# Folding a two-layer network's weights on one core: last pieces by block, and the next stage's first tiles made early

## What is computed

```
h  = gate(LN(x))                        # sigmoid, tanh and cosine of two 512x512 products
for l in 0, 1:
    h = LN(h + (h @ ent_w[l] + ent_b[l]) @ ent_pw[l] + ent_pb[l])       # 512x2048, 2048x512
    h = LN(h + sum_p (h @ path_w[l,p] + path_b[l,p]) * cos/sin factor(phase[l,p]))
```

## Time and profile before

| what | value |
|---|---|
| median of 3 runs | 1646.76 us (1643.83 to 1646.97) |
| the profiled execution: time | 1646.83 us |
| the profiled execution: span | 1644.8 us |
| PE busy | 1490.0 us (91%) |
| PEld busy | 1129.7 us (69%) |
| DVE busy | 1124.7 us (68%) |
| ACT busy | 809.7 us (49%) |
| POOL busy | 539.5 us (33%) |
| mean granted PE clock | 0.956 of 2.4 GHz |

### The profile page before, as it was taken

How to read it: one execution, slowest core, us unless ns; L and a number is a source line. 1 busy time by engine, 2 the same in 40 slices (tenths; PEclk the granted TensorE clock), 3 DMA queues, 4 the chain that set the end, 5 groups by cost and what they waited for, 6 DMA issues and landing times. The chain is left out here.

```text
span 1644.8 us, 26366 instructions
## 1 busy us (share of the span) xinstructions
PE 1490.0 (91%) x8136; PEld 1129.7 (69%) x8136; DVE 1124.7 (68%) x1815; ACT 809.7 (49%) x1723; POOL 539.5 (33%) x593
## 2 busy tenths in 40 slices
PE   4799999999946999999999987999799499898998
PEld 3577777777635777777777766888444278777876
DVE  6788778887526878787878753777558535555556
ACT  4566665566434555555555533555201355545554
POOL 4235324341024554545454513221051331402021
PEclk9899999999977999999999997999899699999999
DMA  4123334324257544454454414000354000000000
GB/s 152 64 90 95 105 107 127 100 84 114 82 174 242 123 115 116 106 124 109 122 108 116 132 27 168 0 0 1 128 204 154 0 1 1 1 27 0 26 26 26
DMA packets 140505, 143.77 MB, mean 87 GB/s; under 512 B 83488, under 2 KB 103072, under 8 KB 138784
## 3 DMA queue, kind: packets, MB, share of 16 engines
q1 hardware_dynamic: 138720, 133.87, 28.2%
q10 hardware_dynamic: 1728, 9.20, 1.7%
HBM read 113.54 MB, written 29.49 MB: 87 GB/s over the span
## 5 line engine op out<-in xcount | busy, mean ns | idle before, releaser
L942 ACT ACTIVATE c_e_t_high<-c_et_ps 128x512 fp32r<-128x512 f32 x128 | 76.7, 599 | 227.4 <-PE c_et_ps L1011 227.4
L820 POOL TENSOR_TENSOR c_mixed_low<-c_whole,c_mixed_high 128x512 fp32r<-128x512 f32 x64 | 96.0, 1500 | 177.1 <-ACT c_mixed_high L954 177.1
L77 DVE TENSOR_TENSOR b_rot_parts_low<-b_rot,b_rot_parts_high 128x1536 fp32r<-128x1536 f32 x64 | 136.0, 2125 | 21.9 <-ACT b_rot_parts_high L526 21.9
L1003 PE MATMUL c_sc_ps<-c_kv_t,c_q 128*128 128x257 f32 x512 | 136.6, 391 | 13.7 <-DMA c_q<-carried_queries 13.7
L843 DVE TENSOR_REDUCE c_peak<-c_sc_ps 128x2 f32<-128x514 f32 x128 | 88.5, 692 | 55.0 <-PE c_sc_ps L1003 54.3
L264 POOL TENSOR_TENSOR b_turned_raw<-b_turn_part 128x384 f32<-128x384 f32 x32 | 70.1, 2189 | 167.7 <-DVE b_key_parts_low L77 166.5
L1003 PEld LDWEIGHTS c_sc_ps<-c_kv_t,c_q 128*128 128x128 f32 x512 | 99.6, 196 | 33.1 <-DMA c_q<-carried_queries 14.6
L309 DVE TENSOR_TENSOR b_rot<-b_w_qr,b_angle 128x1536 f32<-128x1536 f32 x64 | 119.2, 1863 | 0.2
L1515 PE MATMUL f_ps<-f_right,f_left 128*128 128x512 f32 x256 | 112.5, 601 | 7.3 <-POOL spare L1487 5.0
L934 ACT ACTIVATE c_e<-c_sc_ps,c_peak 128x257 f32<-128x257 f32 x256 | 118.8, 475 | 0.0
L70 PE MATMUL c_out_ps<-c_w_vo_high,c_mixed_high 128*128 128x512 f32 x256 | 112.0, 437 | 3.3 <-POOL c_mixed_low L820 3.3
(11 more groups left out here) (211 smaller groups left out, 3876.3 us busy)
## 6 DMA issues: line engine op xcount, KB each, us to landing
c_q<-carried_queries SPq DMA_DIRECT2D x64, 256.0 KB, 3.7
c_ends_spread<-end_weights SPq DMA_DIRECT2D x64, 256.0 KB, 4.3
carried_queries<-x SPq DMA_DIRECT2D x7, 2048.0 KB, 11.2
b_early<-early SPq DMA_DIRECT2D x15, 640.0 KB, 3.9
c_raw<-cache_t SPq DMA_DIRECT2D x64, 128.5 KB, 3.8
c_swapped<-cache_t SPq DMA_DIRECT2D x128, 64.2 KB, 3.8
f_left<-ent_in SPq DMA_DIRECT2D x16, 512.0 KB, 5.5
f_right<-ent_out SPq DMA_DIRECT2D x16, 512.0 KB, 6.7
```

Of the source, the lines that this page charges most:

```text
L77: return nc.vector.tensor_tensor(low, value, high.bitcast(F32), ALU.subtract)
L820: nc.gpsimd.tensor_tensor(mixed[1][:, w, :, u], whole[:, u % 2].rearrange("p (h s) -> p h s", h=H), mixed[0][:, w, :, u].bitcast(F32), ALU ...
L1003: last = nc.tensor.matmul(sc_ps[:, 2 * half + c, 0:L], q[:, u, at], kv_t[:, u], start=True, stop=True)
```

## The change

Seven edits:

1. The block `root_deviations` for x2 is gone; ACT's root and DVE's inverse are the first instructions of `fold_weights`.
2. In `fold_weights`, PE does pieces 0 to 5 as before, and pieces 6 and 7 block by block: for each m the four last steps k, then a signal `block_done`. ACT copies a block when it is done, and copy and rounding alternate block by block. DVE's `finish` starts on a block when that block is copied, and makes the low part of block m - 1 behind the three instructions of block m. PE starts block m of layer 1 when block m of layer 0 is copied. The slots of pieces 6 and 7 come free with the fourth `block_done`.
3. The six bias rows are no longer spread over 128 partitions and added at the end. POOL clears `acc` (128 x 2048), SP then loads each row into one partition of `acc` (six DMAs of 2 KB), and PE's spreading matmul adds them with the rest. Four of them are multiplied by their phase row on one partition (DVE, 1 x 512 each) ahead of the second half of layer 0's sum. `keep_bias` is one copy. DVE's first sum step now waits for the root and for all six rows, the first step is a multiply-add like the others, and the two memsets of `acc` are gone.
4. Only the four phase rows are spread (1 MB).
5. POOL normalises the four tiles of the feed-forward's first turn at the start of the fold (eight instructions of 128 x 512), ahead of its wait for `modulated`.
6. In the feed-forward the input tiles come first on ACT and DVE, and the gate weights are rounded and split in eight blocks of 128 x 4 x 128; each gate result waits only for its own block. The tanh starts behind all eight splits.
7. A tile of the self attention shares the memory of `bias`; the tile `e_xn` lives since before the fold.

The core of the diff:

```diff
 SP, fold_weights
-            sp.dma_start(row[:] ..., rows[0:NR] ... .to_broadcast([P, NR * D])).then_inc(rows_loaded, 16)
+            sp.wait_ge(cleared, 1)
+            for j, at, r in places:
+                sp.dma_start(acc[at:at + 1, j], rows[r:r + 1]).then_inc(rows_loaded, 16)
+            sp.dma_start(phases[:] ..., rows[PH:PH + MODS] ... .to_broadcast([P, MODS * D])).then_inc(phases_loaded, 16)
...
-                        sp.wait_ge(piece_used, turn - SLOTS + 1)
-                        sp.wait_ge(accumulated, (turn - SLOTS + 1) * KQ)
+                        old = turn - SLOTS
+                        if old % PIECES < WHOLE:
+                            sp.wait_ge(piece_used, WHOLE * (old // PIECES) + old % PIECES + 1)
+                        else:
+                            sp.wait_ge(block_done, CD * (old // PIECES + 1))
+                        sp.wait_ge(accumulated, (old + 1) * KQ)
 POOL, fold_weights
-            nc.gpsimd.memset(ones, 1.0).then_inc(pool_chained, 1)
+            nc.gpsimd.memset(acc, 0.0).then_inc(cleared, 1)
+            nc.gpsimd.memset(ones, 1.0).then_inc(ones_set, 1)
+            pool.wait_ge(inverted, 1)
+            gate.normalise_first(nc, pool, x2, stat)
             pool.wait_ge(modulated, 1)
 PE, fold_weights
-            pe.wait_ge(pool_chained, 1)
             for l in range(LAYERS):
-                for q in range(PIECES):
+                for q in range(WHOLE):
...
+                for m in range(CD):
+                    for k in range(WHOLE * KQ, CF):
+                        if m == 0 and k % KQ == 0:
+                            arrived(l, k // KQ)
+                        last = multiply(l, k, m)
+                    last.then_inc(block_done, 1)
 ACT, fold_weights
+            nc.scalar.activation(stat[:, 1], stat[:, 1], ACT.Sqrt, bias=eps[:], scale=1.0 / D).then_inc(rooted, 1)
...
             for n, j in enumerate(STAGES):
-                if j % 2 == 0:
-                    act.wait_ge(piece_used, PIECES * (j // 2 + 1))
-                    for m in range(CD):
+                for m in range(CD):
+                    if j % 2 == 0:
+                        act.wait_ge(block_done, CD * (j // 2) + m + 1)
                         nc.scalar.activation(raw[:, 0, m], ps[:, m], ACT.Copy).then_inc(copied, 1)
-                for m in range(CD):
                     act.wait_ge(gained, CD * n + m + 1)
                     nc.scalar.activation(folded[0][:, j, m], raw[:, j % 2, m], ACT.Copy).then_inc(rounded, 1)
 DVE, fold_weights (order at the start)
+            dve.wait_ge(rooted, 1)
+            nc.vector.reciprocal(stat[:, 1], stat[:, 1]).then_inc(inverted, 1)
             dve.wait_ge(loads.col_loaded, 16)
+            dve.wait_ge(rows_loaded, 16 * len(places))
             sum_entangled(0, range(SLOTS * KQ))
-            dve.wait_ge(rows_loaded, 16)
+            dve.wait_ge(phases_loaded, 16)
...
+            for l in range(LAYERS):
+                for p in range(PW):
+                    at = slice(32 * p, 32 * p + 1)
+                    nc.vector.tensor_tensor(acc[at, 2 * l + 1], acc[at, 2 * l + 1], phases[at, l * PW + p], ALU.mult).then_inc(rows_weighed, 1)
+            dve.wait_ge(rows_weighed, MODS)
             sum_entangled(0, range(SLOTS * KQ, CF))
 feed_forward
-            normalise_tiles(0)
             normalise_tiles(1)
...
-                if f == 0:
-                    pe.wait_ge(weights_split, which + 1)
+                pe.wait_ge(weights_split, r + 1)
...
-            round_weights(0, angle)
             for u in range(G):
                 round_input(0, u)
-            round_weights(1, sigma)
+            for which, raw in enumerate((angle, sigma)):
+                for f in range(CD):
+                    round_weights(which, f, raw)
             act.wait_ge(preset, 1)
-            act.wait_ge(weights_split, 2)
+            act.wait_ge(weights_split, 2 * CD)
```

More of the change, by code:

```diff
@@ L1432, in first, with fold_weights @@
         sp.dma_start(self.paths[:], self.path[0]).then_inc(self.paths_loaded, 16)
-def fold_weights(nc, loads, path, rows, spare, half_pi, ident, folded, bias, out_norm, gate):
-    PB, PH = LAYERS, LAYERS + LAYERS * PW
+def fold_weights(nc, loads, path, rows, x2, stat, eps, spare, half_pi, folded, bias, out_norm, ident, gate):
+    PH = LAYERS + LAYERS * PW
     with ExitStack() as ctx:
@@ L1448, in fold_weights @@
         raw = sb("f_raw", [P, 2, CD, D])
-        turns = raw[:, 0, 0:LAYERS * PW]
-        row = sb("f_row", [P, NR, D])
+        turns = raw[:, 0, 0:MODS]
+        phases = sb("f_phases", [P, MODS, D])
         acc = spare[:, 0:2 * LAYERS * D].rearrange("p (j d) -> p j d", j=2 * LAYERS)
@@ L1454, in fold_weights @@
         bias_ps = ctx.enter_context(nc.psum_tensor("f_bias_ps", [P, 2 * LAYERS, D], F32))
[L1455 to L1459, removed]
+        phases_loaded, norm_loaded, rows_loaded, rows_weighed = (sem(f"f_{n}") for n in ("phases_loaded", "norm_loaded", "rows_loaded", "rows_weighed"))
+        ones_set, cleared, rooted, inverted, pool_chained, summed = (
+            sem(f"f_{n}") for n in ("ones_set", "cleared", "rooted", "inverted", "pool_chained", "summed"))
+        chained, cosined, modulated, piece_used, block_done, copied = (
+            sem(f"f_{n}") for n in ("chained", "cosined", "modulated", "piece_used", "block_done", "copied"))
+        accumulated, spread, gained, rounded, split = (sem(f"f_{n}") for n in ("accumulated", "spread", "gained", "rounded", "split"))
         block = ctx.enter_context(nc.Block())
@@ L1500, in _, with multiply @@
         def _(pe):
+            def multiply(l, k, m):
+                slot = k % (SLOTS * KQ)
+                if l and k == 0:
+                    pe.wait_ge(copied, CD * (l - 1) + m + 1)
+                return nc.tensor.matmul(ps[:, m], left[:, slot, m * P:(m + 1) * P], right[:, slot], start=k == 0, stop=k == CF - 1)
             def spread_bias(j, n):
@@ new lines, in _ @@
+            dve.wait_ge(loads.col_loaded, 16)
+            dve.wait_ge(rows_loaded, 16 * len(places))
+            sum_entangled(0, range(SLOTS * KQ))
+            dve.wait_ge(phases_loaded, 16)
+            flat = lambda a: a.rearrange("p r d -> p (r d)")
+            link(nc.vector.tensor_scalar(phases[:], phases[:], PI / 4, None, ALU.subtract))
+            link(nc.vector.tensor_scalar(turns, phases[:], 1.0 / (2 * PI), MAGIC, ALU.mult, ALU.add))
+            link(nc.vector.tensor_scalar(turns, turns, MAGIC, None, ALU.subtract))
@@ L1646, in feed_forward @@
         minus_quarter = sb("e_minus_quarter", [P, 1])
-        xn = sb("e_xn", [P, G, D])
+        xn = gate.tiles
         xn_t = pair("e_xn_t", [P, CD, T])
@@ L1934, in _ @@
             dve.wait_ge(loaded, 48)
-            split_weights(0, angle)
             for u in range(G):
                 split_input(0, u)
-            split_weights(1, sigma)
+            for which, raw in enumerate((angle, sigma)):
+                for f in range(CD):
+                    split_weights(which, f, raw)
             apply_gates(0)
@@ L2010, in perceiver_block @@
             loads = FoldLoads(nc, fold_scope, paths, ent_in, ent_out, path, columns)
[L2011 to L2013 removed]
+            self_attention(nc, x1, stat, holo, basis_t, bias, ident, loads)
+            fold_weights(nc, loads, path, rows, x1, stat, eps, spare, half_pi, folded, bias, out_norm, ident, gate)
         feed_forward(nc, x1, stat, gate, spare, folded, bias, out_norm, eps, half_pi, ident, out)
```

106 lines of the change are left out of this document (50 added, 56 removed).

## The result

The changed kernel took 1631.46 us in the median of 4 runs (1631.01 to 1632.9), the kernel before 1646.87 beside it (1643.83 to 1650.29). The medians differ by 15.4 us; the ratio is 0.9903, interval 0.9885 to 0.9922, which is 12.8 to 18.9 us faster. 1637.5 was forecast, in a range of 1625.5 to 1643. The profiled execution took 1631.73 with a span of 1629.8; the one before had 1644.8.

What follows compares the result with a forecast made beforehand. The path through PE's start, the change of layer, the tail and the feed-forward's start bounds the kernel. 6.9 us later, less 9.95, less 6.3 gives -9.3: from 1646.83 to 1637.5 us, range 1625.5 to 1643.

Steps and rivals of the forecast that it cites:

- the likeliest case: Whole kernel: PE stalls 5 to 14 us at the change of layer, time 1631 to 1642; chance 0.65.
- the wait it named: Change of layer: PE idle for 5 to 14 us in layer 1's first four multiplications, with the clock falling.
- A: Fold's start: PE begins 0.65 us behind the self attention's last copy, at 1167.25; 2.3 us gained.
- C: Tail from PE's last fold matmul to the feed-forward's block: 15.4 us becomes 5.45, gain 9.95.
- D: Feed-forward's start, block to first gate matmul: 13.3 us becomes 7.0, gain 6.3 (range 5.3 to 6.8).
- B: Change of layer: a late DVE and POOL chain holds PE; its last fold matmul comes 6.9 us later.
- B, the steps: Fold's start: DVE's eight sum steps, 6.3 us alone, lose about 4.7 beside POOL's tiles; over at 1183.8.
- B, at PE: Layer 1's fourth multiplication gets its copy 9.4 us late, restart adds 2.1; last fold matmul at 1292.8.
- Edits at nothing: Fold: shared memory, `block_done` and slots freed up to 6.9 us later cost nothing; layer 1's first piece lands just in time.
- Rival 1: Change of layer: no stall, DVE and POOL early or not holding each other; gain 20.9, 1625.9 us; chance 0.17.
- Rivals 3 and 4: Longer low clock or tiles holding the first gate, 1644 us, chance 0.13; late row loads, slower than before, chance 0.05.

Runs made afterwards that it cites:

- e8: The kernel before with only the x2 deviations block removed, root and inverse standing first in the fold; ratio 0.9967 to the kernel before.
- e1: Changed kernel with POOL's second pass over paths held until layer 0's four copies are made; ratio 0.9901 to the kernel before.
- e2: Changed kernel with ACT copying all four blocks of layer 0 before rounding any; ratio 0.9879 to the kernel before.
- e7: Changed kernel with tiles at the end of POOL's fold list, POOL's second pass behind the fourth copy, ACT's layer 0 copies first; ratio 0.9906.
- e9: Changed kernel with tiles last in POOL's fold list, ACT's layer 0 copies first, DVE's first eight layer 1 steps ahead of finish(1); 1621.95 us.

## Why the prediction was right, and where it was off

The time lay in the range and just inside the likeliest case (1631 to 1642), 6.0 under the forecast. The mechanism was the forecast's: the trace shows the wait it named, at that place, with the clock falling. The size of the whole was not: 15 us were gained where 9.3 was forecast. Half of the difference is stretches whose code the change left alone.

- **A**: 2.6 gained where 2.3 was put; e8 shows it alone. The step that was off is PE's start, 0.33 behind E and not 0.65.
- **C**: 9.92 against 9.95. The parts were right one by one.
- **D**: 6.61 against 6.3, first gate 6.67 behind the block and not 7.0.
- **B**: +4.5 at T1 against +6.9, the term most mis-sized. The rows landed 5.0 behind E, not 6.2: POOL's memset started 0.3 behind E (0.5 forecast), six issues took 1.77 (2.3), and DVE's first step began 1.15 behind them (1.6).
- **B, the steps**: DVE's steps lost 3.5 and not 4.7, although they ran beside POOL's tiles for 7.6 us and not 4.8. I priced the tiles' holding too high; where both engines alternate a tile instruction reads 1.37 to 1.48. Steps were over at E + 14.8 (17.2 forecast), DVE free at E + 51.6 (53.6), POOL's second pass over at E + 61.8 (63.7). All four 1 x 512 multiplications were over with POOL's third instruction, where the forecast had one left.
- **B, at PE**: the fourth multiplication of layer 1 began at E + 67.2 (69.8 forecast), and from there to T1 it took 56.6 (56.4, with 2.25 of low clock and not 2.1). So the 2.4 at the head of the chain, 1.9 of which were left behind POOL's second pass, came to 2.6 at PE and 2.4 at T1. PE itself could have begun that multiplication at about E + 59.6 (60.4). It was 7.6 late and not 9.4: 6.1 of idle, and 1.5 by which the second and third multiplication took longer, a term that the forecast did not have.
- **Edits at nothing**: the fifth piece was in time in the changed kernel only because PE was late itself. The prediction named that cover for the first piece of layer 1; e1, e2 and e7 show it for the fifth: with PE earlier, the piece was 2.0 to 5.4 us late.
- **The rest**: of the 5.65 us between the spans' difference (-15.0) and the sum (-9.35), 2.4 is B, 0.3 is D, 0.9 is E, and 2.06 is the stretch behind the gate. No run isolates the last two: e8, with that stretch as before, took 328.86 there and the others 327.65 to 328.75, so at most 1.2 us of it come with the change and the rest is how one execution differs from another.
- **Rival 1** (no wait) did not come about here but describes e9: its T1, 114.7 behind E, was met with 113.85. What was said for it did not hold, since POOL's tiles did slow DVE. **Rivals 3 and 4** did not come about: the low clock of the change of layer was over before 1240, and the rows came early.

What gives POOL its turn between the four multiplications stays open. That the rows lie in two quadrants (groups of 32 partitions) was the prediction's reason, and no run put them in one. In the earlier trace rows three steps that all start at partition 0 took turns with POOL in the same way. But each step waits for the one before to end, and the multiplications don't.

The Trainium skill, page SBUF — State Buffer, section "SBUF: two separate sides", has another: a VectorE instruction with two SBUF inputs, or one in a two-port mode, and a GpSimd one that reads SBUF exclude each other on one pair of ports, each for its whole length. The trace agrees with that in the held rows above, of which L1604 (4.68) has only one tensor input and would be of the second kind; no run shows its mode. By this rule each of the three multiplications can be as long as the POOL instruction beside it without quadrants. It was not tried apart from the other rule.

## What to carry to other kernels

When a change makes a producer's blocks early, look at the order in which the consumer's program takes them. ACT's copy, round, copy handed DVE's delay to PE, and four copies first undid it (6.0 us). Work put on an idle engine is not free: POOL's tiles held DVE's steps, and 3.2 of the 3.5 us that this cost reached T1. After a wait is removed, list what is late next and move that too. e7 shows three remedies worse than one; in e9, with an earlier release of a slot, T1 comes 9.9 us earlier.

## What the hardware showed that I had not expected

- Eight DVE steps of 128 x 512 took 9.73 us beside POOL instructions of the same size and 6.27 alone; beside POOL's matrix instructions (4.9 us each) a DVE instruction of 0.49 took 4.68, and one on a single partition 4.89, where the first of its kind had taken 0.68. In these rows the price goes by the length of POOL's instruction and not by DVE's own size.
- A short wait of PE can cost more than its length, and a longer one need not. In e2 PE's last 64 records took 29.43 us behind a wait of 1.99, in e9, without one, 27.63: the wait cost 3.8 in all. In e7 they took 29.74 behind a wait of 5.35. But in the kernel before the wait of 2.31 at the change of layer left the granted clock at 1.00, as the windows below show, and in e8 too. What decides between these cases isn't shown. Windows of the kernel before, around that wait and from there to T1 (columns as above):

```profile
1226.00:1236.00 10.00, 7.69 (x19) 3.23 (x18) 6.78 (x14) 4.59 (x8) 0.00 (x0) 1.00 0.32 105
1236.00:1286.00 50.00, 50.00 (x118) 22.15 (x117) 38.90 (x59) 5.15 (x9) 4.62 (x1) 1.00 0.33 126
```

- The end of the unchanged code ahead of the fold moved between 1162.4 and 1170.7 us over the profiled executions. With that scatter an edit worth 3.4 us shows in the stretches and not surely in the total.
